# The first batch's key blocks written by VectorE instead of GpSimd, with new order tables, in a fused two-layer block

## The reference

```python
# layer 0: cross attention to the context, 16 heads of 16
xq, xkv = ada_ln(x, cond, Wss_q), ada_ln(ctx, cond, Wss_kv)
q, (k, v) = xq @ Wq + bq, split(xkv @ Wkv + bkv)
x = x + softmax(q k^T / 4) v @ Wp + bp
# layer 1: prototypes, a router over 3 experts, a gate
nx = layer_norm(x); evidence = softmax(nx Wq (ctx Wk)^T / 16) (ctx Wv)
combined = [nx, evidence, cond]
probs = softmax(combined @ router_W + router_b)
h = silu(combined @ e_w1[e] + e_b1[e])          # 3 experts, 768 -> 512 each
routed = sum_e probs[e] * (h @ e_w2[e] + e_b2[e])
g = sigmoid(silu(combined @ gate_w1 + gate_b1) @ gate_w2 + gate_b2)
x = x + g * (routed @ out_w + out_b)
```

## Time and profile before

| | us |
|---|---|
| runs of before | 436.37, 436.40, 435.59 (median 436.37) |
| profiled execution, time | 436.02 |
| profiled execution, span from first to last instruction | 434.0 |
| PE busy | 413.0 |
| DVE busy | 326.9 |
| POOL busy | 205.5 |
| mean granted TensorE clock, share of full speed | 0.994 |

### The profile page before, as it was taken

The page is one execution under the profiler, slowest core; times in us unless marked ns, Lnnn a source line. Parts: engine busy times, 40 slices in busy tenths (PEclk is TensorE's granted clock), DMA queues, the critical chain, the costliest instruction groups (busy, mean ns, idle before and its releaser), DMA issues.

```text
span 434.0 us, 6956 instructions
## 1 busy us (share of the span) xinstructions
PE 413.0 (95%) x2319; PEld 322.8 (74%) x2319; DVE 326.9 (75%) x814; ACT 211.4 (49%) x372; POOL 205.5 (47%) x322
## 2 busy tenths in 40 slices
PE   7988888889999999999999999999999999999995
PEld 5766554566656666755789889898888898989985
DVE  7688868887897888689958788779568575565662
ACT  3756837655674563663423735563423655521220
POOL 4277868877753234101257332453454234265255
PEclk9999989999999999999999999999999999999999
DMA  8922411313200200001100000001000100001001
GB/s 274 400 60 87 145 36 40 95 36 87 60 15 12 74 12 14 1 2 42 39 1 2 0 2 1 2 0 50 1 2 1 50 0 2 2 0 50 0 2 48
DMA packets 8179, 18.93 MB, mean 44 GB/s; under 512 B 1009, under 2 KB 2545, under 8 KB 8017
## 3 DMA queue, kind: packets, MB, share of 16 engines
q1 hardware_dynamic: 7200, 15.55, 10.9%
q0 software_dynamic: 656, 2.29, 2.0%
q10 hardware_dynamic: 288, 0.66, 0.4%
HBM read 13.97 MB, written 2.10 MB: 37 GB/s over the span
## 4 chain that ended last, share of the span: by engine, by line
PE 76%; DVE 12%; issue 4%; POOL 4%; DMA 2%; ACT 1%; POOLq 0%; SPq 0%; DVEq 0%
PE bank L1364 47%; PE pair L1364 16%; PE pair L1502 3%; DVE nm L1102 3%; POOL xq L670 3%; PE bank L1536 2%; DVE xq L1119 2%; PE bank L1533 2%; DMA wss_sb<-in_wss 2%; PE bank L1384 1%; DVE kc L1063 1%; PE bank L1548 1%; DVE xh L1012 1%; DVE lnt L994 1%; PE bank L1655 1%
## 5 line engine op out<-in xcount | busy, mean ns | idle before, releaser
L723 POOL TENSOR_TENSOR hs<-hid,hs 128x512 fp32r<-128x512 f32 x48 | 64.1, 1342 | 85.3 <-DVE hs L1281 85.2
L926 ACT ACTIVATE hid<-bank,ab 128x512 f32<-128x512 f32 x56 | 38.4, 688 | 81.2 <-PE bank L1364 60.3
L1364 PE MATMUL bank<-nx,w1h 128*128 128x512 f32 x224 | 71.6, 401 | 0.0
L1364 PE MATMUL pair<-w2h,hs 128*128 128x256 f32 x384 | 70.5, 283 | 0.0
L1102 DVE TENSOR_REDUCE nm<-pair 128x4 f32<-128x616 f32 x64 | 51.0, 796 | 18.3 <-PE pair L1502 17.3
L1364 PEld LDWEIGHTS pair<-w2h,hs 128*128 128x128 f32 x384 | 60.6, 189 | 1.8
L1364 PE MATMUL pair<-w2l,hs 128*128 128x256 f32 x192 | 54.2, 282 | 0.0
L857 ACT ACTIVATE pt<-bank 128x512 f32<-128x512 f32 x72 | 40.7, 597 | 25.2 <-PE bank L1364 24.4
L1364 PEld LDWEIGHTS bank<-nx,w1h 128*128 128x128 f32 x224 | 39.4, 189 | 6.6 <-ACT hid L926 0.3
L1364 PE MATMUL bank<-wh,m_ev 128*128 128x512 f32 x112 | 44.1, 394 | 0.0
L1364 PE MATMUL bank<-nx,w1l 128*128 128x512 f32 x112 | 44.1, 394 | 0.0
(11 more groups left out here) (215 smaller groups left out, 888.3 us busy)
## 6 DMA issues: line engine op xcount, KB each, us to landing
xq<-xq SPq DMA_DIRECT2D x15, 128.0 KB, 2.3
stage<-in_w1n POOLq DMA_DIRECT2D x7, 256.0 KB, 3.1
w1e_sb<-in_w1e SPq DMA_DIRECT2D x1, 1792.0 KB, 6.9
x_sb<-in_x SPq DMA_DIRECT2D x3, 512.0 KB, 8.8
stage<-in_w1a SPq DMA_DIRECT2D x3, 512.0 KB, 11.1
stage<-in_ew2T SPq DMA_DIRECT2D x3, 512.0 KB, 4.0
out_x<-x_sb SPq DMA_DIRECT2D x3, 512.0 KB, 2.7
wss_sb<-in_wss SPq DMA_DIRECT2D x2, 512.0 KB, 6.8
```

Of the source, the lines that this page charges most:

```text
L723: g_.tensor_tensor(hs[:, q % 3, 1, :], hid[:, (M1 * c + HORD.index(m)) % 2, :], hs[:, q % 3, 0, :], ALU.subtract).then_inc(hl_r, 1)
L926: A(hid[:, n % 2, :], B_H[n % 2][:, :], ACT.Silu, bias=ab1[:, m, c // CPB:c // CPB + 1]).then_inc(h_r, 1)
L1364: ins = mm(dst, a, b_, start=first and i == 0, stop=last and i == len(terms) - 1, skip_group_check=free)
```

## The change

The step `kr` moves from GpSimd's walk to VectorE's. `row_keys`, `tail_keys` and `place` are written again in the block of VectorE with the same shapes; the copy of `place` there has no wait for its own last result. GpSimd keeps its copies of `row_keys` and `tail_keys` for the second batch and waits there for both semaphores, which two engines now raise. One wait in the step `scale` on VectorE is dropped. (A second, identical `shift` appears in GpSimd's block.) Both order strings are new.

```diff
@@ gpsimd
-            def place(gi):
-                pool.wait_ge(kg_r, gi + 1)
-                pool.wait_ge(k2_r, gi + 1)
-                for j in (0, 1):
-                    row_keys(0, gi, gi + 1, j)
-                for s_ in range(2):
-                    tail_keys(0, gi, gi + 1, s_)
-                pool.wait_ge(kt_r, 2 * gi + 2)
             def second(i):
                 pool.wait_ge(prep_r, 1 + PI[("k", 1)])
                 pool.wait_ge(k2_r, 2 * NG)
+                pool.wait_ge(kr_r, 2 * NG)
+                pool.wait_ge(kt_r, 2 * NG)
@@ vector
+            def row_keys(b, g0, g1, j):
+                V.tensor_scalar(kr[b][:, g0:g1, LK * j:LK * j + LK], kc[b][:, g0:g1, j // 2, 0:LK], sm("mkey", j), None,
+                                ALU.mult).then_inc(kr_r, 1)
+            def tail_keys(b, g0, g1, s_):
+                V.tensor_tensor(kt[b][:, g0:g1, s_, :].rearrange("p g (j n) -> p g j n", j=GH),
+                                kc[b][:, g0:g1, s_, P:KP].unsqueeze(2).broadcast_to([P, g1 - g0, GH, 32]),
+                                sm("mtail", GH * s_, GH).unsqueeze(1).unsqueeze(3).broadcast_to([P, g1 - g0, GH, 32]),
+                                ALU.mult).then_inc(kt_r, 1)
+            def place(gi):
+                dve.wait_ge(kg_r, gi + 1)
+                dve.wait_ge(k2_r, gi + 1)
+                for j in (0, 1):
+                    row_keys(0, gi, gi + 1, j)
+                for s_ in range(2):
+                    tail_keys(0, gi, gi + 1, s_)
             def scale(j):
-                dve.wait_ge(pr_r, NC)
                 dve.wait_ge(th_r, TJ * (NC - 1) + j + 1)
@@ order strings, first lines
         EARLY_ORDER = (
-            "sfqcPsQQbfrbPJVIfRVrcRgIfRJQfRnSQfrrRfKKRfKPnRKbfIRPKSJfA"
-            "KKbRfKKRxyIfKRsxRSJfA"
-            "sRKfgKPKRyfKPIRyKRSnJfA"
+            "sqscQQfrPbPIJfVVRIfbgRfJcRQfRrnfSRQfRnKfRrKrKKPRKSfIPJfbKA"
+            "KKRIfyKRfKRxJRA"
+            "SbRgsfKxRKKsKRKfPIPnRfSJyyA"
...
         L1_ORDER = (
-            "iH"
-            "jkBH"
+            "BH"
+            "H"
```

More of the change, by code:

```diff
@@ L378, in build @@
             "A": [("av", g) for g in range(GR)],
+            "y": [("second", n) for n in range(6)],
             "x": [("xt", c, h) for c in range(1, NC) for h in range(2)],
-            "y": [("second", n) for n in range(6)],
             "u": [("uz", n) for n in range(TJ * NC)],
@@ L383, in build @@
             "w": [("wp", n) for n in range(TJ * NC)],
+            "t": [("m_taken", n) for n in range(len(MP))],
             "m": [("m", n) for n in range(len(MP))],
-            "t": [("m_taken", n) for n in range(len(MP))],
             "L": [("ln_stats", c) for c in range(NC)],
@@ L438, in build @@
[L438 to L460, removed]
@@ L484, in build @@
-            "GH"
-            "aXH"
-            "DDUhhhaeeDeeD"
+            "ikH"
+            "jhLhH"
+            "GhllDhH"
+            "NhDGLNFiUH"
+            "DCUH"
+            "EUDhhCEGUH"
+            "WH"
+            "WhCDTCWEDWTDEH"
+            "TBGhUThUDpH"
+            "lUiUH"
+            "H"
+            "lNhhojDhNH"
+            "jBhH"
+            "DFDH"
+            "CH"
+            "hCUUZZUDEUH"
+            "H"
+            "GZDWhWEH"
+            "ZTCDBhEDhCUEUDH"
+            "LUH"
@@ new lines, in build @@
+            "H"
+            "UhWGhlBH"
+            "WDhGDTTpDH"
+            "hUDUUThUlH"
+            "GNoH"
+            "hDDFjNjH"
+            "BDhH"
+            "CCH"
+            "UEWDH"
+            "UhhEUUH"
+            "hWZDThCDZZH"
+            "hCZH"
+            "EDGH"
+            "DH"
+            "H"
+            "BUUUTUWhEDhGDDBWhTGH"
+            "hpDH"
+            "ThUUUUH"
+            "H"
+            "GjBH"
+            "hDUjUUDhZDDhH"
+            "H"
+            "H"
@@ L487, in build @@
+            "UhGoZDH"
+            "H"
+            "ZDH"
+            "hDZBH"
+            "hhUDGUH"
+            "DH"
+            "UDUBhhGBH"
+            "hhUDDXaXUH"
+            "H"
+            "UUhaahGXDaDDXeDeee"
         )
@@ L663, in second, with shift @@
                     pool.wait_ge(kt_r, 2 * NG + i - GH + 1)
+            def shift(g):
+                pool.wait_ge(nt_r, g + 1)
+                for a in range(TJ):
+                    r = slice(32 * a, 32 * a + 32)
+                    g_.tensor_copy(xq[SHIFT, g % 2].rearrange("p s (q a t) -> p s q a t", q=TJ, a=TJ)[:, :, :, a, :],
+                                   nt[r, g % 2].unsqueeze(1).broadcast_to([32, 2, TJ, 32])).then_inc(sh_r, 1)
+                pool.wait_ge(sh_r, TJ * (g + 1))
             def shift(g):
@@ L711, in _ @@
             pool.wait_ge(x4_r, B)
-            walk(EARLY_STEPS, {"parts": parts, "kr": place, "second": second, "prep": prep, "hi": hi, "shift": shift, "xt": xb, "keys": keys, "av": av, "rsqrt": newton, "ln_stats": lambda c: newton(NC + c)})
+            walk(EARLY_STEPS, {"parts": parts, "second": second, "prep": prep, "hi": hi, "shift": shift, "xt": xb, "keys": keys, "av": av, "rsqrt": newton, "ln_stats": lambda c: newton(NC + c)})
             pool.wait_ge(m_h, m_hi(MTAIL))
```

65 lines of the change are left out of this document (21 added, 44 removed).

## The result

| | before | after |
|---|---|---|
| runs, median us | 436.22 (4 runs) | 431.40 (4 runs: 431.06, 430.29, 431.75, 431.98) |
| ratio, 95% interval | | 0.9889 [0.9865, 0.9913] |
| profiled execution, time / span | 436.02 / 434.0 | 431.06 / 429.2 |

The kernel became 4.8 us faster. The direction was right, the size was not.

The account below looks back on a forecast made before the run. VectorE was the fullest engine in the open first 130 us, PE nearly full afterwards. Terms -1.35 - 0.75 + 0.3 + 0.2 + 0.3 = -1.3 us on 436.02 gave 434.7, with 0.35 for the runs' median 435.1; range 431.8 to 439.4.

Parts of the forecast that it names:

- The start: Start of the kernel: key projection becomes PE's first product; of VectorE's 1.51 us wait for its parts, 1.0 credited.
- Placing on VectorE: First stretches: 16 more VectorE instructions, 4.9 us of durations, cost 4.0 us of its time, ends 3.5 and 8.2.
- GpSimd's relief: First stretches: GpSimd loses 8.8 us of placing, taken as worth 0 on the path, at most 1.57 us.
- Idle time of VectorE that the new head fills: Up to the transpose of g = 3: 1.0, 1.7 and 3.4 us of VectorE's 10.2 idle us get filled.
- the hole: PE idle for 1.65 us until 59.13, after late GpSimd casts at g = 2; without it the clock was expected to stay up.
- `norm2,0` ahead of the transpose: Before the transpose of g = 3: two more VectorE instructions, about 0.75 us, paid back after it as -0.75.
- From there to 207.5 us both lists have the same work; single steps are exchanged: From the transpose of g = 3 to 207.5 us: the lead stays except 0.3 us given back where PE is full.
- End of layer 0 and layer 1: `hidden(0, 13)` may start some 0.2 us later: +0.2; layer 1, without PE idle time: +0.3, between -1 and +3.
- (a): Rival, start: VectorE is the bound, its holes don't fill, and the clock drops again; +2.5, 438.9 us; chance 0.20.
- (b): Rival: the start's lead or lag is absorbed, PE being nearly full from 133 us; no change, 436.4 us; chance 0.22.
- (c): Rival, start: GpSimd was the better part of the trouble; late casts, half clock and holes go; 432.6 us; chance 0.12.
- (d): Rival, start: placing is blocked by GpSimd's casts and copies, 3.3 us more less 1 of idle time; 437.4 us; chance 0.10.

Follow-up runs that it names:

- unblocked order: Changed kernel with `norm2,0` moved behind `shift3` and `norm2,1` from behind `rows4,2` to behind `rows4,1`: 429.50 us; with placing on GpSimd as well, 430.15 us.
- four moves: Kernel before with only `split2,1`, `norm3,0`, `norm3,1` and `split3,0` moved a place or two in VectorE's list, to where GpSimd has nothing: 435.34 us.
- move only: Changed kernel with both order strings of the kernel before, so the old order with placing on VectorE: 441.08 us.
- placing done twice: Changed kernel in which VectorE writes each of the 16 key blocks once more, to a place overwritten later: 434.93 us.

## Why the forecast was too small, point by point

**The start** (credit 1.0): right, 1.08 us (18.46 against 19.54).

**Placing on VectorE** (4.0, ends 3.5 and 8.2): 3.3 us, a little under the lower end. The durations were as forecast (0.29 us each against 0.31 and 0.30), 4.7 us in all. But such instructions start 0.20 us apart, so their overlap is worth 1.4 us, not the 0.9 that I took off. None was held up in the changed kernel. The rule of the Trainium skill, "SBUF — State Buffer", section "Who interferes with whom" (the one that has the shared ports holds them for its whole instruction), is borne out where the two engines do meet: a `tensor_scalar` of the placing took 1.17 instead of 0.30 us beside a memset, and a two-input tail 0.70 instead of 0.28 beside a cast that reads (0.90 for a pair that takes 0.49). Both kinds can be held up, then; in the changed kernel they stand where they meet nothing.

**GpSimd's relief** (0): right, to within 0.5 us. With the placing on GpSimd the new order is as fast (430.59 beside 430.31, with the old layer 1). The unblocked order is 429.50 with the placing on VectorE and 430.15 with it on GpSimd, on two chips: 0.3% of ratio that the marks don't explain.

**Idle time of VectorE that the new head fills** (1.0 + 1.7 + 3.4 = 6.1 of 10.2 us): right. From 16.8 to 65.0 us VectorE is busy for 16.82 + 7.15 + 10.74 + 9.27 = 44.0 of 48.2 us, idle for 4.2, so 6.0 were filled. Busy time rose by 3.7 (forecast 4.75), and the transpose of g = 3 came 2.4 us earlier (forecast 1.35), which is 1.0 us of the miss. That the clock stays up without the hole was right too, though it can stay up with it ("four moves"). That mending the hole is worth something by itself was not: without it, the kernel before takes 436.13.

**`norm2,0` ahead of the transpose** (0.75 us, repaid): it took 1.67 us for its two instructions, since a bias add of GpSimd started 0.05 us after it. Putting both norms elsewhere is worth 1.1 to 1.4 us from the first key part to g = 15.

**"From there to 207.5 us both lists have the same work; single steps are exchanged", give back 0.3.** This step failed. By the marks, the part behind g = 3 holds +1.5, -3.7 and -0.4: -2.6 us where the forecast has -0.75 and +0.3. "The same work" was right for VectorE's list, and it was no argument: the stretch from g = 5 to 11 was not bound by an amount of work. VectorE was busy for 46.8 of 55.6 us there, 3.8 of that in excess time of instructions held up beside GpSimd's. I had called only the first 130 us open and then read no order behind g = 3, although I had quoted a blocked cast of that very stretch, only as a bound for the placing. I had also counted VectorE's list up to the transpose of g = 3, but not GpSimd's, in which the new order has two blocks of the second batch less by then (`second1`, `second2`). What the runs showed in its place: GpSimd in time for the casts of g = 2 and 3, 1.7 us; most blocked instructions of VectorE gone, 0.8 us; and a rest of about 2.5 us. For this rest it is shown where it arises (g = 5 to 11) and that it needs both halves of the new order. Up to 1.0 us of it may be further blocking, and that the remainder comes from where PE's side products stand is argued, not shown; no single step of it was found, so its cause stays open.

**End of layer 0 and layer 1** (+0.2, +0.3): -0.1 (29.6 against 29.7 us) and +0.3 by the windows, but nothing by the run with the old layer 1. Both are within what can be told.

**The rivals.** (a), VectorE as the bound, is what the move does in the old order (441.1) and what a second placing does in the new one (434.9); the new tables prevent it. (b), the lead absorbed, is what happens when only the head is new (435.2). It does not happen in the changed kernel, whose lead at g = 15 is larger than at g = 3. (c), GpSimd as the better part of the trouble, gave the nearest number, 432.6, by a cause that is shown for 1.7 us only, and of that the clock and the first hole are nothing without the second one. (d), blocked placing, appears in the move alone (0.8 us).

## What to carry to other kernels

When a new order comes with a moved step, run the order without the move: here the order was the whole gain, and the move, in the old order, a loss of 5.4 us that the new one covers. Compare two orders beyond the place that you understand: look for instructions far above the shortest of their kind, and see what the neighbouring engine does beside each; they are cheap to move. An engine that is late at one point may be late at the next one for another reason, as GpSimd was here, so freeing one wait can show nothing until the second is gone too; and here a lead was kept only where what came next wasn't short of room too.

## What the runs showed of the hardware

Back to back, the placing's VectorE instructions start closer together than they last: 0.29 us each, 0.20 us apart.

What is held up, and beside what, in these traces: a `tensor_scalar` of 128x256 floats took about 1.15 instead of 0.40 us when a 0.95 us memset of GpSimd began just after it, and 0.82 to 1.0 beside a two-input add; a cast of 128x512 took 1.28 instead of 0.42 beside the memset; a two-input subtraction took 1.10 instead of 0.69 beside a two-input add of GpSimd. The row maxima, which read TensorE's results, stayed at 0.80 us beside memsets, casts and adds alike (not more than 0.04 us above the shortest, in eight of these kernels), and so did the `low` parts (0.75 us), which have one input from `bank`. By the profile, GpSimd's memset begins 0.04 to 0.1 us after VectorE's instruction (91.34 after 91.30, 43.22 after 43.12) and still isn't the one that is held up, which was not expected; GpSimd's spans are rough in the profile.

The granted clock fell to its half level (1.2 GHz) for 3.4 us each time after or at the end of an idle stretch of PE: of 1.65 us before 59.13 (before, clock down at 60.4), of 1.62 us before 41.49 (move only, 42.5) and of 3.58 us before 47.91 (placing done twice, 47.7). Such a stretch doesn't always bring the drop: the clock stayed up after 1.65 us before 59.58 ("four moves") and after 2.00 us before 26.46 (move only). Near 60 us it did not fall in any profiled execution without that hole.
